# A graph network on one core: layer-norm statistics of two tiles in one VectorE instruction, and three steps of the first layer's edge stage moved from ScalarE to VectorE

## The reference, cut to what matters

```python
def _layernorm(x, axis=-1, eps=1e-05):
    m = jnp.mean(x, axis=axis, keepdims=True)
    v = jnp.var(x, axis=axis, keepdims=True)
    return (x - m) / jnp.sqrt(v + eps)

h = jnp.maximum(_layernorm(x, axis=-1), 0.0)
x = x + _L0_gnn_ref(h, edge_index, L0_gnn_W)          # tanh of a normed, degree-weighted edge sum
h = jnp.maximum(_layernorm(x, axis=-1), 0.0)
x = x + _L1_gnn_ref(...)                              # two relational attention layers, 8 edge types
h = jnp.maximum(_layernorm(x, axis=-1), 0.0)
x = x + _L2_gnn_ref(...)                              # equivariant edge products
h = jnp.maximum(_layernorm(x, axis=-1), 0.0)
x = x + _L3_gnn_ref(...)                              # layer norm again, two groups of attention heads
```

## Time and profile before

| what | value |
|---|---|
| median of 3 runs | 4019.06 us (4015.88 to 4021.55) |
| profiled execution, time | 4020.56 us |
| profiled execution, span of its instructions | 4018.8 us |
| PE busy | 3075.4 us, 77% |
| DVE busy | 3290.3 us, 82%, 9625 instructions |
| ACT busy | 2173.0 us, 54% |
| POOL busy | 2085.5 us, 52% |
| DMA | 679.72 MB, mean 169 GB/s |

### The profile page before, as it was taken

How to read it: one execution, slowest core, us unless ns; L and a number is a source line. 1 busy time by engine, 2 the same in 40 slices (tenths; PEclk the granted TensorE clock), 3 DMA queues, 4 the chain that set the end, 5 groups by cost and what they waited for, 6 DMA issues and landing times. The chain is left out here.

```text
span 4018.8 us, 66244 instructions
## 1 busy us (share of the span) xinstructions
PE 3075.4 (77%) x13334; PEld 1749.4 (44%) x13334; DVE 3290.3 (82%) x9625; ACT 2173.0 (54%) x5748; POOL 2085.5 (52%) x2017
## 2 busy tenths in 40 slices
PE   4866757777749997569995658999979999218886
PEld 1255644444424443124442545555546666104443
DVE  6979979999969997768786877888956666779997
ACT  0048868999952322442221776777746666115554
POOL 5945557766637551037660006666645555006676
PEclk9967778999969998889997888999989999659998
DMA  2069987877742221689993994555545565213332
GB/s 56 3 189 311 308 268 234 253 246 245 246 118 74 69 69 36 183 226 278 282 276 103 287 268 108 143 143 142 137 148 194 197 199 190 68 46 112 114 113 86
DMA packets 635184, 679.72 MB, mean 169 GB/s; under 512 B 168901, under 2 KB 496159, under 8 KB 628581
## 3 DMA queue, kind: packets, MB, share of 16 engines
q1 hardware_dynamic: 587012, 575.17, 45.7%
q0 software_dynamic: 48000, 102.76, 11.6%
HBM read 385.35 MB, written 296.91 MB: 170 GB/s over the span
## 5 line engine op out<-in xcount | busy, mean ns | idle before, releaser
L1411 PE MATMUL r_pM<-r_masked,wr 128*128 128x512 f32 x1600 | 712.8, 596 | 10.7 <-DVE r_masked L1356 10.7
L1356 DVE SCALAR_TENSOR_TENSOR r_masked<-r_typ,r_hT 128x512 f32<-128x512 f32 x800 | 495.4, 690 | 101.7 <-ACT r_hT L1389 78.7
L1411 PEld LDWEIGHTS r_pM<-r_masked,wr 128*128 128x128 f32 x1600 | 295.4, 191 | 357.4 <-issue 291.9
L691 POOL DMA_INDIRECT q_rows<-nr,row_x x200 | 259.2, 1296 | 194.8 <-PE q_pT L600 134.5
L2432 POOL DMA_INDIRECT out<-o_base,o_at_o x200 | 266.1, 1331 | 134.4 <-issue 66.3
L691 POOL DMA_INDIRECT r_xs<-h_tab,r_at_s x200 | 229.9, 1149 | 87.7 <-issue 47.0
L691 POOL DMA_INDIRECT r_xs<-tab,r_at_s x200 | 212.1, 1060 | 87.9 <-issue 46.5
L691 POOL DMA_INDIRECT e_zd<-xz,dst_c x200 | 191.7, 959 | 90.4 <-issue 52.6
L691 POOL DMA_INDIRECT i_hs<-hr,i_at_s x200 | 191.3, 957 | 87.8 <-issue 47.1
L2240 ACT ACTIVATE q_eo<-q_pO,b 128x512 f32<-128x512 f32 x196 | 134.7, 687 | 172.5 <-PE q_pO L2275 148.8
L691 POOL DMA_INDIRECT e_zs<-xz,src_c x200 | 190.4, 952 | 71.0 <-issue 59.1
(11 more groups left out here) (426 smaller groups left out, 9141.8 us busy)
## 6 DMA issues: line engine op xcount, KB each, us to landing
xz<-na_xz SPq DMA_DIRECT2D x49, 1040.0 KB, 5.8
r_typ<-vec_s SPq DMA_DIRECT2D x100, 256.0 KB, 4.5
g_al<-alpha_s SPq DMA_DIRECT2D x100, 256.0 KB, 4.3
na_xz<-in_x SPq DMA_DIRECT2D x49, 512.0 KB, 6.9
tab<-na_x SPq DMA_DIRECT2D x49, 512.0 KB, 2.8
e_xin<-tab SPq DMA_DIRECT2D x49, 512.0 KB
hr<-e_hh SPq DMA_DIRECT2D x49, 512.0 KB, 3.2
nr<-e_n SPq DMA_DIRECT2D x49, 512.0 KB
```

Of the source, the lines that this page charges most:

```text
L691: pool.indirect_dma_start(dest[:, j, :], None, table, bass.IndirectOffsetOnAxis(ap=index[:, j:j + 1], axis=0), element_offset=first).then_ ...
L1356: v.scalar_tensor_tensor(masked[:, r, :], typ[d.slot(4)][:, :], float(r), hT[d.slot(2)][:, :], ALU.is_equal, ALU.mult).then_inc(ev.mk, 1)
L1411: pe.matmul(pM[s][:, :], g.wr[:, layer * R_ + r, :], masked[:, r, :], start=(r == 0), stop=(r == R_ - 1)).then_inc(ev.mm, 1)
```

## The change

stats now takes any even number of tiles. One bn_stats reads two tiles in turns, value 0 of the first, value 0 of the second, value 1 of the first and so on, so that the even half of its six numbers belongs to the first tile and the odd half to the second. bn_aggr, pair_stats, the wait between them and the buffers of the six numbers are gone; users read the mean at [1] and count times variance at [2], which is scaled by 1/128 in rstd (L587) and at L877. For e_z the eight tiles lie in two PSUM banks, and each instruction stays within one bank.

In layer0_edges VectorE takes over from ScalarE the relu e_hTx (after the statistics of e_z, with its waits on the transposes), the copy e_pq (after the statistics of e_x, with its waits on the product in pX and on the store of two blocks before) and the two tiles of e_n; e_nr and the semaphores nd.n0 and nd.nr go, with SP's wait on nd.n0.

```diff
@@ -571,27 +571,23 @@
-def stats(v, c, g, x4, st, mv, done):
+def stats(v, x, mv, done):
+
+    for j in range(0, x.shape[1], 2):
+        last = v.bn_stats(mv[:, j:j + 2, :].rearrange("p t c -> p (t c)"), x[:, j:j + 2, :].rearrange("p t f -> p f t"))
+    last.then_inc(done, 1)
+
+
+def rstd(a, g, c, mv, rs, done):
+
+    c.step(a.activation(rs[:, :], mv[:, :, 2], ACT.Ln, bias=g.eps_ln[:, :], scale=1.0 / P))
+    a.activation(rs[:, :], rs[:, :], ACT.Exp, scale=-0.5).then_inc(done, 1)
+
+
+def normalise(v, x4, mv, rs, y4, done):
 
     for j in range(J):
-        last = v.bn_stats(st[:, j, :], x4[:, j, :])
-    c.step(last)
-    v.sem_inc(g.state.waits, 1)
-    for j in range(J):
-        last = v.bn_aggr(mv[:, j, :], st[:, j, :])
-    last.then_inc(done, 1)
-
-
-def rstd(a, g, c, mv, rs, done):
-
-    c.step(a.activation(rs[:, :], mv[:, :, 1], ACT.Ln, bias=g.eps_ln[:, :]))
-    a.activation(rs[:, :], rs[:, :], ACT.Exp, scale=-0.5).then_inc(done, 1)
-
-
-def normalise(v, x4, mv, rs, y4, done):
-
-    for j in range(J):
-        last = v.tensor_scalar(y4[:, j, :], x4[:, j, :], mv[:, j, 0:1], rs[:, j:j + 1], ALU.subtract, ALU.mult)
+        last = v.tensor_scalar(y4[:, j, :], x4[:, j, :], mv[:, j, 1:2], rs[:, j:j + 1], ALU.subtract, ALU.mult)
     last.then_inc(done, 1)
...
-
-def pair_stats(v, c, g, x8, st, mv, done):
-
-    for j in range(2 * J):
-        last = v.bn_stats(st[:, j, :], x8(j))
-    c.step(last)
-    v.sem_inc(g.state.waits, 1)
-    for j in range(2 * J):
-        last = v.bn_aggr(mv[:, j, :], st[:, j, :])
-    last.then_inc(done, 1)
...
-            c = Chain(v, s_v, 2 * SLOTS)
+            c = Chain(v, s_v, SLOTS)
...
-                    pair_stats(v, c, g, lambda j: rows[:, j, 0:P], st, mv[s], ev.st)
+                    stats(v, rows[:, :, 0:P], mv[s], ev.st)
                     v.wait_ge(ev.st, p.one())
                     v.wait_ge(ev.rs, p.one_back(2))
-                    v.tensor_scalar(ve[s][:, :], mv[s][:, :, 1], EPS_LN, None, ALU.add).then_inc(ev.ve, 1)
+                    v.tensor_scalar(ve[s][:, :], mv[s][:, :, 2], 1.0 / P, EPS_LN, ALU.mult, ALU.add).then_inc(ev.ve, 1)
                 d = pair(5)
...
         hh, n_ = some("hh", 4, [P, 2 * J, P]), some("n", 4, [P, 2 * J, P])
-        stz, sth = (sb(n, [P, 2 * J, 6]) for n in ("stz", "sth"))
-        mvz, mvh = (sb(n, [P, 2 * J, 2]) for n in ("mvz", "mvh"))
+        mvz, mvh = (sb(n, [P, 2 * J, 3]) for n in ("mvz", "mvh"))
...
-        nr = sb("nr", [P, J])
...
         z = [ctx.enter_context(nc.psum_tensor(f"e0_z{k}", [P, 2, HW], F32)) for k in range(2)]
         z_tile = lambda p, j: z[p.slot(2)][:, j // J, j % J * P:(j % J + 1) * P]
+        z_tiles = lambda p, j: z[p.slot(2)][:, j // J, j % J * P:(j % J + 2) * P]
...
-        BY_ACT = 2
...
                 p = pair(3)
                 if p:
                     s = p.slot(4)
-                    wait_alone(g, sp, nd.n0, p.one())
                     for table, rows, done, stored in ((g.hr, hh, nd.hh, w_h), (g.nr, n_, nd.nn, w_n)):
...
                 if n1:
                     v.wait_ge(nd.z, n1.now())
                     v.wait_ge(nd.nm, n1.one_back(1))
-                    pair_stats(v, c, g, lambda j: z_tile(n1, j), stz, mvz, nd.sz)
+                    for j in range(0, 2 * J, 2):
+                        last = v.bn_stats(mvz[:, j:j + 2, :].rearrange("p t c -> p (t c)"), z_tiles(n1, j).rearrange("p (t f) -> p f t", t=2))
+                    last.then_inc(nd.sz, 1)
+                if e3:
+                    v.wait_ge(ed.tx, e3.now())
+                    v.wait_ge(ed.pq, e3.back(1))
+                    v.tensor_scalar(hTx[:, :], pX[:, :], 0.0, None, ALU.max).then_inc(ed.hx, 1)
                 if n2:
                     v.wait_ge(nd.hh, n2.now())
                     v.wait_ge(nd.nn, n2.one_back(1))
-                    pair_stats(v, c, g, lambda j: hh[n2.slot(4)][:, j, :], sth, mvh, nd.sh)
+                    stats(v, hh[n2.slot(4)], mvh, nd.sh)
                 if e2:
                     s = e2.slot(4)
                     v.wait_ge(ed.r2, e2.now())
@@ -1104,28 +1091,31 @@
                         v.wait_ge(w_x[s], 16 * e2.uses(4))
                     v.scalar_tensor_tensor(x1[s][:, :, :], zd[e2.slot(4)][:, :, 0:P], 1.0, et[:, :, :], ALU.add, ALU.subtract).then_inc(ed.x1, 1)
                     v.wait_ge(ed.x1, e2.now())
-                    stats(v, c, g, x1[s], sx, mx, ed.sx)
+                    stats(v, x1[s], mx, ed.sx)
+                if e3:
+                    v.wait_ge(ed.pq, e3.now())
+                    if e3.k >= 2:
+                        v.wait_ge(w_q[e3.slot(2)], 16 * e3.uses(2))
+                    v.tensor_copy(pq[e3.slot(2)][:, :], pX[0:R_, :]).then_inc(ed.pe, 1)
                 if n2:
                     s = n2.slot(4)
                     v.wait_ge(nd.rh, n2.one())
                     if n2.k >= 4:
                         v.wait_ge(w_n[s], 16 * n2.uses(4))
-                    v.wait_ge(nd.n0, n2.one_back(1))
-                    v.scalar_tensor_tensor(nr[:, :], mvh[:, of(0), 0], -1.0, rh[:, of(0)], ALU.mult, ALU.mult).then_inc(nd.nr, 1)
-                    for j in range(BY_ACT, 2 * J):
-                        last = v.tensor_scalar(n_[s][:, j, :], hh[s][:, j, :], mvh[:, j, 0:1], rh[:, j:j + 1], ALU.subtract, ALU.mult)
+                    for j in range(2 * J):
+                        last = v.tensor_scalar(n_[s][:, j, :], hh[s][:, j, :], mvh[:, j, 1:2], rh[:, j:j + 1], ALU.subtract, ALU.mult)
                     last.then_inc(nd.nn, 1)
                 if n1:
                     v.wait_ge(nd.rz, n1.one())
                     v.wait_ge(nd.hh, n1.back(1))
-                    v.scalar_tensor_tensor(nm[:, :], mvz[:, :, 0], -1.0, rz[:, :], ALU.mult, ALU.mult).then_inc(nd.nm, 1)
+                    v.scalar_tensor_tensor(nm[:, :], mvz[:, :, 1], -1.0, rz[:, :], ALU.mult, ALU.mult).then_inc(nd.nm, 1)
             braid.written_out(turn)
...
                         a.wait_ge(w_h[s], 16 * n2.uses(4))
                     a.wait_ge(nd.nn, n2.one_back(4))
-                    a.wait_ge(nd.n0, n2.one_back(4))
...
-                if e3:
-                    a.wait_ge(ed.tx, e3.now())
-                    a.wait_ge(ed.pq, e3.back(1))
-                    a.activation(hTx[:, :], pX[:, :], ACT.Relu).then_inc(ed.hx, 1)
...
-                if e3:
-                    a.wait_ge(ed.pq, e3.now())
-                    if e3.k >= 2:
-                        a.wait_ge(w_q[e3.slot(2)], 16 * e3.uses(2))
-                    a.activation(pq[e3.slot(2)][:, :], pX[0:R_, :], ACT.Copy).then_inc(ed.pe, 1)
-                if n2:
-                    s = n2.slot(4)
-                    a.wait_ge(nd.nr, n2.one())
-                    if n2.k >= 4:
-                        a.wait_ge(w_n[s], 16 * n2.uses(4))
-                    for j in range(BY_ACT):
-                        last = a.activation(n_[s][:, j, :], hh[s][:, j, :], ACT.Identity, scale=rh[:, j:j + 1], bias=nr[:, j:j + 1])
-                    last.then_inc(nd.n0, 1)
             braid.written_out(turn)
...
-                    stats(v, c, g, xs[n1.slot(4)], st, mv[n1.slot(2)], ev.st)
+                    stats(v, xs[n1.slot(4)], mv[n1.slot(2)], ev.st)
...
-                    stats(v, c, g, rows[d.slot(4)], st, mv[s], ev.st)
+                    stats(v, rows[d.slot(4)], mv[s], ev.st)
...
-                    stats(v, c, g, x3[s], st, mv, ev.st)
+                    stats(v, x3[s], mv, ev.st)
                 d = at(5)
                 if d:
                     v.wait_ge(ev.hh, d.now())
                     v.wait_ge(ev.nn, d.back(1))
-                    stats(v, c, g, hh[d.slot(2)], sth, mvh, ev.sh)
+                    stats(v, hh[d.slot(2)], mvh, ev.sh)
```

More of the change, by code:

```diff
@@ L885, in turn @@
                         v.wait_ge(ev.t1, p.back(1, m))
-                        v.tensor_tensor(y[:, of(m), :], rows[:, of(m), 0:P], mv[s][:, of(m), 0:1].broadcast_to([P, J, P]), ALU.subtract).then_inc(ev.ya, 1)
+                        v.tensor_tensor(y[:, of(m), :], rows[:, of(m), 0:P], mv[s][:, of(m), 1:2].broadcast_to([P, J, P]), ALU.subtract).then_inc(ev.ya, 1)
                 p = pair(3)
@@ L985, in layer0_edges @@
         hTx = sb("hTx", [P, HW])
-        sx, mx = sb("sx", [P, J, 6]), sb("mx", [P, J, 2])
+        mx = sb("mx", [P, J, 3])
         rx, nn, ss, ssw, ri, q = (sb(n, [P, J]) for n in ("rx", "nn", "ss", "ssw", "ri", "q"))
@@ L1127, in _ @@
             c = Chain(a, s_a)
-            braid.credit(a, ed.cp, ed.ss, ed.ri, ed.r2, ed.rx, ed.hx, ed.pe, nd.rz, nd.rh, nd.n0)
+            braid.credit(a, ed.cp, ed.ss, ed.ri, ed.r2, ed.rx, nd.rz, nd.rh)
             braid.credit_pairs(a, nd.hh)
@@ L1363, in turn @@
                     v.tensor_tensor(z[s][:, :, :], z[s][:, :, :], hh[p.slot(2)][:, :, :], ALU.add).then_inc(zz, 1)
-            line.sweep(v, turn, c)
+            line.sweep(v, turn)
         @block.scalar
@@ L1699, in aggregate_rows @@
         rows, hh = some("rows", 4, [P, J, P]), some("hh", 2, [P, J, P])
```

(8 more changed lines are left out.)

15 lines of the change are left out of this document (5 added, 10 removed).

## The result

The changed kernel takes 3949.73 us (median of 4 runs, 3947.92 to 3955.88) against 4017.47 us for the kernel before in the same comparison: ratio 0.9833, interval 0.9816 to 0.985. It is 1.7% faster, where I had forecast 4054 us, slower than before, and a range whose lower end was 3958 us. The experiments ran on five chips. On three the kernel before takes 4020 to 4025 us, much as here; on two it takes 4193 and 4196 us, and there the change gains nothing. The second set of single instructions ran on one of the two; only those instructions are used of it, and those it shares with the first set last as long in both.

The account below looks back on a forecast made before the run. VectorE was taken to bound layer0_edges, with DMA as full as VectorE in node_rows. layer0_edges +50 us and node_rows -15 us gave +35 us on 4020.6, 4055.6, set to 4054 us; 8-in-10 range 3958 to 4072 us.

Parts of the forecast that it names:

- the price of one instruction for two tiles: A bn_stats on 256 alternating values: 0.522 us with a jump surcharge, 0.333 us as the other end.
- the sign that this step is wrong: A bn_stats on two tiles lasting under 0.5 us would refute going from scattered rows to the alternating read.
- The two surcharge rows: Two scattered-read instructions in the trace before, L376 (16-byte steps) and L1560 (800-byte steps), each 0.74 ns more a value.
- VectorE's list runs without a hole: In layer0_edges VectorE's instructions follow each other without idle time, so VectorE sets the 11.02 us turn.
- (A): Rival: jumps are free, 0.333 us a pair; layer0_edges -22 us, node_rows -26 us, total 3971 us; chance 0.36.
- The half: In node_rows, if jumps are free, DMA lets through half of the 52 us saving, -26 us.
- its bound of 15: aggregate_rows: VectorE waits for a load at DMA share 0.99; bounds 0 and -15 us, forecast 0.
- The moves: layer0_edges: relu 0.68, copy 0.68 and two e_n tiles 0.51 us added to VectorE, 1.87 us a turn.
- no hole: layer0_edges: transposes finish at 911.11, before VectorE reaches the relu at 911.64, so the relu adds no wait.
- interaction: This stage gains nothing: shorter statistics only lengthen the scan's wait for i_pL; bound 0 to 0.37 us.
- relations: This stage gains nothing: TensorE is full, 382 of 390 us, and the statistics hide under its products.

Follow-up runs that it names:

- The second set of single instructions: The change plus a short stage of single bn_stats, on SBUF and PSUM: three places 0.45 us, a 12-byte step 0.49 us, four places in PSUM 0.43 us.
- the probes: The change plus a short stage of single VectorE instructions on 256 values in different read orders: neighbours and two places 0.43 us, 16-byte step 0.61 us.
- e3: The kernel before, old statistics kept, with relu e_hTx, copy e_pq and two e_n tiles moved to VectorE: 4128.36 us, ratio 1.0256.
- e2_stats_only: The changed kernel with relu e_hTx, copy e_pq and two e_n tiles back on ScalarE: 3935.43 us, ratio 0.9776, against 4024.97 us for the kernel before.

## Why the prediction was wrong

**The step that failed** is the price of one instruction for two tiles: "I take 0.522 us, because the new reads also jump with every value". The row shows 0.333 us, and each instruction lasts 0.416 us, under the 0.5 us that I had named as the sign that this step is wrong. The two surcharge rows were read rightly, and the probes repeat them; but they read from many places or at a step of 16 bytes, and the change reads from two. "L1560 comes back to each neighbourhood after eight reads and isn't spared" was true, and eight isn't two. Ten instructions a turn at 0.189 us too much are 1.89 us a turn, 93 us, and in node_rows four are 37 us before the transfers bound it. With this price alone put right the sum would be 3925 us (4019 - 42 - 52), so a second step failed too: that VectorE's list runs without a hole. Of these 94 us 58 came in the two stages, because the ring holds e_x back and the transfers hold node_rows, the two limits that (A) named.

No row of before shows a read that alternates between two places; that it would pay at every value was my estimate. The probes put the orders side by side: the alternating read jumps 512 bytes at every value and takes 0.43 us as the straight one, a step of 8 bytes takes 0.43 us too, a step of 16 bytes 0.61 us, four places 0.59 us.

**Rival (A)** gave 3971 us (3945 to 3997); 3949.7 lies in it. layer0_edges: -22 us, measured -23.3, -0.48 us a turn instead of -0.44. Size and mechanism were right: e_x starts right behind e_et in 39 of 50 turns. (A) took e_et at its old time and came to -0.44 us; the ring closes at 10.50 us instead of the 11.02 us of the earlier trace rows. What (A) didn't have is the wait before the relu, 28.2 us in all, which in those turns only takes up time that e_x would have waited. node_rows: -26 us by half of 52, measured -34.7; the transfers could still rise from 311 to 345 GB/s, and there they stopped. The half was a guess, and that it came near is luck. The other stages: 0, measured -13 us in small parts, 3.4 of them where nothing was changed; aggregate_rows gave 4.6 of its bound of 15.

**The moves:** 1.87 us a turn, measured 2.07, and that this is near is luck in part: relu and copy were priced at 0.68 us each, their whole durations, where 0.61 and 0.59 us from start to start would have been due, and the wait before the relu was put at nothing ("no hole") where e3 shows 0.65 us a turn, with the old statistics. With the new ones VectorE waits there 0.18 and 1.26 us in the two turns before and of the timeline above, 0.56 us in the mean of 50.

**interaction** went as forecast: VectorE's busy time fell from 456 to 412 us, and its idle time before the scan rose from 34.8 to 78.5 us, all for i_pL. The first and the last scan are 504.2 us apart, 502.9 before. relations likewise kept its length.

**The range** ended at 3958 us because I let it take in only part of (A), whose own lower end was 3945, and gave (A) 0.36. With the deciding price open between two ends and nothing in the trace between them, the range had to hold both whole.

## What to carry to other kernels

Read a surcharge together with its pattern: how many places an instruction alternates between and at what step; the two rows here agreed on 0.74 ns a value and said nothing of a third pattern, which paid none. Statistics of two tiles in one bn_stats start 0.333 us apart where those of a single tile start 0.199 us apart and bn_aggr comes on top, and alone they brought 90 of 4025 us (e2_stats_only): worth trying where VectorE sets the pace. And the steps to move to the engine that comes free should be tried singly, since here the three together gave back some 14 us of what the statistics had brought. Ask of each step whether it lies on a loop of waits between the engines: here the two that did cost time, though the engine that took them had idle time left. When several moves leave a turn unchanged, look for a floor they share, and for a second one right behind it.
